# Edge stage of a graph-attention and mixture-of-experts kernel: each gather of source rows waits for the landing of the last but one

## The chip, the core and the metric

The kernel is one program on one core of a Trainium2 chip. A core has five engines that run their own instruction streams and meet through semaphores: PE (TensorE, matmuls), DVE (VectorE), ACT (ScalarE), POOL (GpSimd) and SP (SyncE, which here only issues DMAs); 16 DMA engines move the data. The metric is the device time of one execution in microseconds, lower is better.

## What is computed

A graph layer and a mixture of experts follow each other. Cut to what matters:

```
x = x + gnn(layernorm(x), ...)                       # 3750 nodes x 256, 120000 edges sorted by dst
    feat_all = einsum('ni,rhid->rnhd', inputs, conv_weights)       # 8 relations, 4 heads of 64
    feat_src_e = feat_all[edge_type, edge_src]                     # one row of 256 per edge
    el, er = attn_l . feat_src_e,  attn_r . feat_dst_e             # per head
    e = leaky_relu(el + er, 0.2)
    alpha = softmax of e over the edges with the same dst
    h = segment_sum(alpha * feat_src_e, edge_dst) + h_bias
x = x + ffn(layernorm(x), ...)                       # top 2 of 8 experts, 256 -> 1024 -> 256, gelu
```

## The kernel before

The program has three stages. The **node stage** (to about 243 us) computes the projected rows of all nodes for all 8 relations and writes them to a table `feats` in DRAM, 30720 rows of 260 floats: 256 features and the 4 left logits, 1040 bytes a row. The **edge stage** (243 to about 1885 us) is where the change lies. The **route and expert stage** follows to the end; it uses no gathers from `feats`.

The edge stage cuts the edges into units of 128 and pairs of two units; a pair adds into one tile of 128 destination nodes, and there are 498 pairs. A group is up to 16 pairs (32 units): `SIZES` is 8, then 30 times 16, then 10, so `GROUPS` = 32. A quad is 4 units. Buffers for groups stand threefold (`GBUFS` = 3, r = g modulo 3), so group g uses the buffer of group g - 3.

Each unit's 128 source rows come by one indirect DMA, issued by POOL (`gather_features`, L798), into `gath[:, r, u]`: 128 x 260 floats, 133 KB. POOL issues them in order of group and unit. Ahead of a group it waits for the indices (`idx_ready`, from `meta_columns` on DVE), and ahead of each quad, from group 3 on, for the sums of the pairs that used the same rows three groups ago (`sum_ready`, `freed(g, j)`). `wait_apart` is a wait followed by an increment of a semaphore `carrier` that nobody reads. Every gather increments `gath_in[r]` by 16 when it has landed; `landed(g, r, n)` is the count that this semaphore has when all of group g is there.

Who waits for the gathers: DVE's `logits(g)` (L838), which adds the left logits, columns 256 to 259 of the gathered rows, to the right logits; and SP, once, before it loads the node rows (L784) for the next stage over the rows of a buffer. DVE's `period(g)` does, in a fixed order, the maxima of group g, the scaling of its first rows by alpha (L905, shared with ACT's L1063), the adding of sums into `acc` (L914), the index work for group g + 3, and ends with `logits(g + 1)`. PE's period turns one-hot matrices (L1113), picks right logits (L1138) and sums (`total`, L1154: `psP` from `hot` and `gath`); totals of group g are spread over period g (its first quads, at the end) and period g + 1 (quads 3 to 7). ACT makes the one-hots. Groups are driven by `each_period`: a few first and last ones written out, the others in a hardware loop of three groups.

SP's loads of edge records, 16 of 12 KB a group, run beside the gathers on SP's own DMA queue.

Of the kernel before, what the change touches and what calls it, by code (L numbers as in the profile page):

```python
# [44 lines left out]
BLK = 2  # L45
# [3 lines left out]
GB = 16  # L49
GU = GB * BLK  # L50
assert GU * HEADS == P
SIZES = [8] + [GB] * ((PAIRS - 18) // GB) + [10]
SHORT = GB - SIZES[0]
# [7 lines left out]
GBUFS = 3  # L61
# [93 lines left out]
def wait_apart(pool, sem, value, carrier):  # L155


    pool.wait_ge(sem, value)
    pool.sem_inc(carrier, 1)
# [14 lines left out]
def load_records(nc, sp, sb, edges, meta, g, landed, of=range(GB)):  # L174

    edge_rows = edges.rearrange("t h c e -> (t h) (c e)")
    for b in of:
        if b % 4 == 0:
            starts = nc.values_load_multi_w_load_instructions(
                sb["pair_row"][0:1, bass.ds(g, 1), b:b + 4].rearrange("a g b -> a (g b)"), engines=(mybir.EngineType.SP,),  # L180
                min_val=0, max_val=(CHUNK_ROWS - BLK) * HEADS)[1]
        at = starts[b % 4]
        sp.dma_start(meta[b * BLK * HEADS:(b + 1) * BLK * HEADS], edge_rows[bass.ds(at, BLK * HEADS), :]).then_inc(landed, 16)
# [441 lines left out]
def edge_stage(nc, sb, edges, feats, xb, wr, br):  # L625
# [6 lines left out]
    with ExitStack() as ctx:  # L632
# [6 lines left out]
        def sem(name):  # L639
            return ctx.enter_context(nc.semaphore(name))  # L640
# [9 lines left out]
        reset, cat, idxT, ndlT, typeT = sb["reset"], sb["cat"], sb["idxT"], sb["ndlT"], sb["typeT"]  # L650
# [24 lines left out]
        SLOTS_Q = GU // QUAD  # L675
        LAG = 3
        PQ = QUAD // BLK

        meta_in = sem("meta_in")
        gath_in = [sem(f"gath_in{r}") for r in range(GBUFS)]  # L680
        rows_ready, rowsT_ready, idx_ready = sem("rows_ready"), sem("rowsT_ready"), sem("idx_ready")
        hot_ready, hotT_ready, hotT_copied, er_done = sem("hot_ready"), sem("hotT_ready"), sem("hotT_copied"), sem("er_done")
        e_ready, eT_ready, spread_ready, lv_ready = sem("e_ready"), sem("eT_ready"), sem("spread_ready"), sem("lv_ready")
# [5 lines left out]
        carrier = sem("carrier")  # L689

        def quads(g):

            if not isinstance(g, int):
                return SLOTS_Q
            return SIZES[g] // PQ if 0 <= g < GROUPS else 0

        def pairs_before(g):
            return BASES[g] if isinstance(g, int) else g * GB - SHORT

        def quads_before(g):  # L700
            return BASES[g] // PQ if isinstance(g, int) else g * SLOTS_Q - SHORT // PQ

# [4 lines left out]
        def landed(g, r, n):  # L707

            if isinstance(g, int):
                return 16 * BLK * sum(SIZES[r:g + 1:GBUFS])  # L710
            return 16 * BLK * GB * (n + 1) - (16 * BLK * SHORT if r == 0 else 0)

        def freed(g, j):

            if isinstance(g, int):
                return BASES[g - GBUFS] + min(PQ * j + PQ, SIZES[g - GBUFS])
            return pairs_before(g - GBUFS) + PQ * j + PQ

        def tiles_of(engine, g, j, n):

            numbers = pair_tile[0:1, bass.ds(g, 1), PQ * j:PQ * (j + n)].rearrange("a g b -> a (g b)")
            return nc.values_load_multi_w_load_instructions(
# [3 lines left out]
        def each_period(eng, body, first, last_loop):  # L726


            for g in range(first):
                body(g, g % GBUFS, g // GBUFS)  # L730
            loops = (last_loop + 1 - first) // GBUFS
            with eng.Fori(0, loops) as i:
                for k in range(first, first + GBUFS):
                    body(i * GBUFS + k, k % GBUFS, i + k // GBUFS)
            for g in range(first + GBUFS * loops, GROUPS + 1):
                body(g, g % GBUFS, g // GBUFS)

        def there(g):
            return not isinstance(g, int) or 0 <= g < GROUPS

        LAST_LOOP = GROUPS - 4
        LAST, LAST2 = GROUPS - 1, GROUPS - 2
        ACT_SCALES = [(LAST2, j) for j in range(3, SIZES[LAST2] // PQ)] + [(LAST, j) for j in range(2, SIZES[LAST] // PQ, 2)]
        ACT_Q = (6, 7)
# [21 lines left out]
        with nc.Block() as block:  # L766
            @block.sync
            def _(sp):
                load_records(nc, sp, sb, edges, meta, AHEAD, meta_in)

                def period(g, r, n):
                    if there(g + AHEAD + 1):
                        sp.wait_ge(rows_ready, g + 1)
                        load_records(nc, sp, sb, edges, meta, g + AHEAD + 1, meta_in)

                each_period(sp, period, 2, GROUPS - AHEAD - 2)
                sp.dma_start(sb["wr_sb"][:], wr.rearrange("(k p) e -> p k e", p=P)).then_inc(sb["small_in"], 16)
                sp.dma_start(sb["br_all"][:], br.to_broadcast([P, EXPERTS])).then_inc(sb["small_in"], 16)

                sp.wait_ge(sum_ready, BASES[LAST2])  # L780
                sp.wait_ge(gath_in[LAST % GBUFS], landed(LAST, LAST % GBUFS, 0))
                x_tiles = xb.rearrange("(t p) f -> p t f", p=P)
                for b, (lo, hi) in enumerate(BATCHES_R):
                    sp.dma_start(rows_of_nodes(sb)[:, lo:hi], x_tiles[:, lo:hi]).then_inc(sb["x_in"][b], 16)  # L784

            @block.gpsimd
            def _(pool):
                def gather_features(g, r, n):
                    if not there(g):
                        return  # L790
                    if not isinstance(g, int) or g >= AHEAD:
                        wait_apart(pool, idx_ready, g - (AHEAD - 1), carrier)
                    for j in range(quads(g)):
                        if not isinstance(g, int) or g >= GBUFS:

                            wait_apart(pool, sum_ready, freed(g, j), carrier)
                        for u in range(j * QUAD, (j + 1) * QUAD):
                            pool.indirect_dma_start(gath[:, r, u], None, feats,  # L798
                                                    bass.IndirectOffsetOnAxis(ap=idxT[:, r, u:u + 1], axis=0)).then_inc(gath_in[r], 16)

                each_period(pool, gather_features, GBUFS + 1, GROUPS - 2)

            @block.vector
            def _(dve):
# [28 lines left out]
                def logits(g, r, n):  # L833

                    dve.wait_ge(picked, g * 2 + 2)
                    dve.wait_ge(gath_in[r], landed(g, r, n))
                    e0 = e_sb[:, 0].rearrange("p (u h) -> p u h", h=HEADS)
                    step(dve.tensor_tensor(e0, gath[:, r, :, D:FW], er_e[:], ALU.add))  # L838
                    dve.scalar_tensor_tensor(e_sb[:, 1], e_sb[:, 0], SLOPE, e_sb[:, 0], ALU.mult, ALU.max).then_inc(e_ready, 1)
# [123 lines left out]
                def period(g, r, n):  # L963
# [53 lines left out]
                    if there(g + 1):  # L1017
                        logits(g + 1, rn, n if r < GBUFS - 1 else n + 1)
# [216 lines left out]
def rows_of_nodes(sb):  # L1235

    words = sb["gath"][:, NODE_BUF].rearrange("p u w -> p (u w)")
    return words[:, 0:TILES * D].rearrange("p (t d) -> p t d", t=TILES)
# [816 lines left out]
```

## Time and profile before

| | |
|---|---|
| time, median of 3 runs | 2474.11 us (2470.37 to 2475.55) |
| span of the profiled execution | 2456.4 us |
| time of the profiled execution itself | not given apart; the runs' median lies 17.7 us above the span |
| busy, share of the span: PE, DVE, ACT, POOL | 77%, 43%, 44%, 46% |
| gathers L798 | 996, 954 ns mean, 950.6 us in total |
| DMA queue of POOL (software_dynamic) | 60192 packets, 149.24 MB |

How to read it: the span is from the first to the last instruction of one execution, taken by the hardware profiler, and busy times are parts of it. The 40 slices give the busy share of each engine in tenths. A timeline row gives start and length of an instruction in microseconds, then engine, line, operation and tiles, and in brackets how long the engine idled before it and what ended that. The length of an L798 row is the time in which POOL issues the gather; the rows land later, as packets of the 16 DMA engines. The landing of a gather has no row of its own.

### The profile page before, as it was taken

The page shows a single profiled execution, that of the slowest core. Times are in us where ns is not written, and L with a number is a line of the kernel's source. Part 1 is how long each engine was busy: PE and PEld are TensorE (multiplying, and loading weights), DVE is VectorE, ACT ScalarE, POOL GpSimd, SP SyncE. Part 2 cuts the span into 40 slices and gives each one's busy share as a digit, 9 for nine tenths or more (in the row PEclk, how much of TensorE's full clock was granted, in tenths as well). Part 3 has the DMA queues.
Part 4 walks back from the last instruction along what each step waited for, and adds up shares of the span by engine and source line. Part 5 has one row for each costly group of instructions (what it writes and reads, how often), then busy time and mean ns, then how long its engine had stood idle before and what let it go on. Part 6 is the DMA issues. An engine that isn't in the chain of part 4 may idle for free. (4 is left out here: it accounts for less than half of the span.)

```text
span 2456.4 us, 35279 instructions
## 1 busy us (share of the span) xinstructions
PE 1898.8 (77%) x9138; PEld 1594.8 (65%) x9139; DVE 1062.3 (43%) x3018; ACT 1076.9 (44%) x3259; POOL 1142.0 (46%) x1164
## 2 busy tenths in 40 slices
PE   8999125767767777867777777677877689999998
PEld 7887124656655665656565666565665668999887
DVE  6332013545555555545555555455567532221111
ACT  2222123645555545554555555454656532222221
POOL 4000744556666566666666566656620443122222
PEclk9999556787877768777787777777788689999999
DMA  6443422333333333333333333333312877777774
GB/s 239 189 170 143 109 67 74 84 90 88 90 92 92 88 88 91 90 88 90 88 92 92 89 90 90 92 85 88 91 44 80 282 230 221 248 246 247 241 234 104
DMA packets 121157, 315.51 MB, mean 128 GB/s; under 512 B 27047, under 2 KB 71335, under 8 KB 106180
## 3 DMA queue, kind: packets, MB, share of 16 engines
q0 software_dynamic: 60192, 149.24, 23.4%
q1 hardware_dynamic: 60836, 164.88, 19.3%
q8 instruction: 41, 0.67, 0.1%
q14 instruction: 88, 0.72, 0.1%
HBM read 257.36 MB, written 57.71 MB: 128 GB/s over the span
## 5 line engine op out<-in xcount | busy, mean ns | idle before, releaser
L798 POOL DMA_INDIRECT gath<-feats,idxT x996 | 950.6, 954 | 799.1 <-issue 272.7
L1154 PE MATMUL psP<-gath,hot 128*128 128x260 f32 x1992 | 668.1, 493 | 28.6 <-DVE gath L905 15.1
L1154 PEld LDWEIGHTS psP<-gath,hot 128*128 128x128 f32 x1992 | 469.4, 247 | 123.5 <-issue 35.4
L1113 PE MATMUL psOT<-cst,hot 128*128 128x128 f32 x996 | 196.1, 331 | 346.0 <-ACT hotT L1045 231.9
L1045 ACT COPY hotT<-psOT 128x512 f32<-128x512 f32 x249 | 143.5, 576 | 628.6 <-remote 485.4
L1113 PEld LDWEIGHTS psOT<-cst,hot 128*128 128x128 f32 x996 | 139.7, 171 | 407.2 <-issue 309.0
L1138 PEld LDWEIGHTS psE<-er,hotT 128*128 128x128 f32 x1992 | 309.7, 235 | 48.6 <-issue 44.9
L914 DVE TENSOR_TENSOR acc<-acc,psP 128x260 f32 x498 | 211.0, 424 | 295.3 <-remote 127.9
L1138 PE MATMUL psE<-er,hotT 128*128 x1992 | 309.5, 305 | 31.1 <-issue 19.9
L1035 ACT ACTIVATE hot<-cst,ndlT 128x128 f32<-128x128 f32 x996 | 316.2, 391 | 4.7 <-PEq L325 4.7
L1680 ACT ACTIVATE acc<-psH,w1buf 128x256 f32<-128x256 f32 (+1 forms) x344 | 122.4, 423 | 346.7 <-PE psH L1571 304.3
L1063 ACT ACTIVATE gath<-gath 128x64 f32<-128x64 f32 x1040 | 261.0, 337 | 0.1
L1496 POOL DMA_INDIRECT out<-acc,node x66 | 103.3, 1565 | 335.0 <-DVE acc L1904 178.0
L1571 PE MATMUL psH<-acc,w1buf 128*128 128x256 f32 (+1 forms) x1376 | 241.9, 334 | 4.4 <-issue 2.4
L1587 PE MATMUL psY<-w2buf,acc 128*128 128x256 f32 x1056 | 240.9, 384 | 3.4 <-issue 3.3
L905 DVE TENSOR_TENSOR gath<-gath,psA 128x1024 f32<-128x1024 f32 x184 | 224.5, 1221 | 27.2 <-ACT gath L1075 19.9
L1571 PEld LDWEIGHTS psH<-acc,w1buf 128*128 128x128 f32 x1376 | 217.8, 194 | 24.8 <-DVE acc L1888 2.9
L585 PE MATMUL psF<-wext,xT 128*128 128x264 f32 x960 | 221.1, 388 | 1.1 <-ACT xT L536 1.1
L1587 PEld LDWEIGHTS psY<-w2buf,acc 128*128 128x128 f32 x1056 | 200.0, 193 | 32.4 <-issue 6.8
L585 PEld LDWEIGHTS psF<-wext,xT 128*128 128x128 f32 x960 | 180.7, 191 | 31.6 <-ACT xT L536 1.5
L1038 ACT ACTIVATE hot<-hot 128x512 f32<-128x512 f32 x249 | 156.8, 630 | 38.3 <-remote 25.9
L1888 DVE TENSOR_SCALAR acc<-psX,w1buf 128x256 f32<-128x256 f32 (+1 forms) x86 | 37.5, 478 | 214.8 <-PE psX L1556 186.1
(232 smaller groups left out, 1178.5 us busy)
## 6 DMA issues: line engine op xcount, KB each, us to landing
w1buf<-in_experts SPq DMA_DIRECT2D x43, 1030.0 KB
w2buf<-in_experts SPq DMA_DIRECT2D x43, 1024.0 KB
feats<-frow SPq DMA_DIRECT2D x29, 1040.0 KB, 3.9
gath<-feats,idxT POOLq DMA_INDIRECT x996
meta<-in_edges SPq DMA_DIRECT2D x464, 12.0 KB
acc<-slots_x SPq DMA_DIRECT2D x23, 258.0 KB
gath<-in_b SPq DMA_DIRECT2D x43, 128.0 KB
acc<-slots_x SPq DMA_DIRECT2D x20, 129.0 KB
```

The lines of the kernel that those rows point to most:

```text
L585: ins = pe.matmul(psF[:, n % BUFS, j, 0:W], xT[:, i % LEAD, k], wext[:, k, 2 * pair + j], start=k == 0, stop=k == KD - 1)
L798: pool.indirect_dma_start(gath[:, r, u], None, feats, bass.IndirectOffsetOnAxis(ap=idxT[:, r, u:u + 1], axis=0)).then_inc(gath_in[r], 16)
L905: dve.tensor_tensor(feat, feat, alpha.unsqueeze(3).to_broadcast([P, QUAD, HEADS, HD]), ALU.mult).then_inc(scaled, 1)
L914: dve.tensor_tensor(into[b % PQ], into[b % PQ], psP[:, bank(g, b, r), 0:FW], ALU.add).then_inc(sum_used, 1)
L1035: ins = act.activation(hot[:, r, u], iota, ACT.Square, bias=ndlT[:, r, u:u + 1])
L1038: act.activation(hot[:, r, j * QUAD:(j + 1) * QUAD], hot[:, r, j * QUAD:(j + 1) * QUAD], ACT.Relu, bias=1.0, scale=-1.0).then_inc(hot_read ...
L1063: ins = act.activation(feat, feat, ACT.Copy, scale=gath[:, r, u, D + h:D + h + 1])
L1113: ins = pe.transpose(psOT[:, k * P:(k + 1) * P], hot[:, r, j * QUAD + k], ident)
L1138: ins = pe.matmul(psE[:, u * W % 512:u * W % 512 + W], hotT[:, j % 2, k * P:(k + 1) * P], tables[k // BLK], start=True, stop=True)
L1154: ins = pe.matmul(psP[:, bank(g, b, r), 0:FW], hot[:, r, u], gath[:, r, u], start=u % BLK == 0, stop=u % BLK == BLK - 1)
L1571: ins = pe.matmul(psH[:, bank(n, g), at * slots(n):(at + 1) * slots(n)], w1(n, k, m), xeT[:, n % 2, k, 0:slots(n)], start=k == 0, stop=k = ...
L1587: ins = pe.matmul(psY[:, y_bank(n, j), 0:D], hT[:, n % 2, m, j * P:(j + 1) * P], w2(n, m), start=m == 0, stop=m == KH - 1)
```

## The change

The semaphore of each buffer becomes two (`FLYING` = 2): gather u raises the one of number u modulo 2. From the third gather of a group on, POOL waits before gather u until the semaphore of that number shows that gather u - 2 of the same group has landed. The first two gathers of a group have no such wait. The counts of `landed` are halved, and DVE and SP wait for both semaphores.

```diff
+        FLYING = 2
-        gath_in = [sem(f"gath_in{r}") for r in range(GBUFS)]
+        gath_in = [[sem(f"gath_in{r}_{q}") for q in range(FLYING)] for r in range(GBUFS)]
...
-                return 16 * BLK * sum(SIZES[r:g + 1:GBUFS])
-            return 16 * BLK * GB * (n + 1) - (16 * BLK * SHORT if r == 0 else 0)
+                return 16 * BLK // FLYING * sum(SIZES[r:g + 1:GBUFS])
+            return 16 * BLK // FLYING * GB * (n + 1) - (16 * BLK // FLYING * SHORT if r == 0 else 0)
+
+        def landed_before(g, r, n):
+
+            if isinstance(g, int):
+                return 16 * BLK // FLYING * sum(SIZES[r:g:GBUFS])
+            return 16 * BLK // FLYING * GB * n - (16 * BLK // FLYING * SHORT if r == 0 else 0)
...
-                sp.wait_ge(gath_in[LAST % GBUFS], landed(LAST, LAST % GBUFS, 0))
+                for q in range(FLYING):
+                    sp.wait_ge(gath_in[LAST % GBUFS][q], landed(LAST, LAST % GBUFS, 0))
...
                         for u in range(j * QUAD, (j + 1) * QUAD):
+                            if u >= FLYING:
+
+                                wait_apart(pool, gath_in[r][u % FLYING], landed_before(g, r, n) + 16 * (u // FLYING), carrier)
                             pool.indirect_dma_start(gath[:, r, u], None, feats,
-                                                    bass.IndirectOffsetOnAxis(ap=idxT[:, r, u:u + 1], axis=0)).then_inc(gath_in[r], 16)
+                                                    bass.IndirectOffsetOnAxis(ap=idxT[:, r, u:u + 1], axis=0)).then_inc(
+                                                        gath_in[r][u % FLYING], 16)
...
-                    dve.wait_ge(gath_in[r], landed(g, r, n))
+                    for q in range(FLYING):
+                        dve.wait_ge(gath_in[r][q], landed(g, r, n))
```

No instruction changes its place; waits are added between them. On POOL, at the head of the hardware loop (a group in buffer 1; `L158` is register and wait work), before:

```order
L158 ISA [waits idx_ready]
L798 DMA gath<-feats,idxT 128x260 [waits sum_ready]
L798 DMA gath<-feats,idxT 128x260 x3
L158 REGISTER_ALU
L798 DMA gath<-feats,idxT 128x260 [waits sum_ready]
L798 DMA gath<-feats,idxT 128x260 x3
```

and now:

```order
L158 ISA [waits idx_ready]
L809 DMA gath<-feats,idxT 128x260 [waits sum_ready]
L809 DMA gath<-feats,idxT 128x260
L158 ISA
L809 DMA gath<-feats,idxT 128x260 [waits gath_in1_0]
L809 DMA gath<-feats,idxT 128x260 [waits gath_in1_1]
L158 REGISTER_ALU
L158 REGISTER_ALU [waits sum_ready]
L809 DMA gath<-feats,idxT 128x260 [waits gath_in1_0]
L809 DMA gath<-feats,idxT 128x260 [waits gath_in1_1]
```

Every gather from the third on has a wait of its own, in turn on the two semaphores of the buffer, where one in four had one. On DVE, the end of a period in the loop, before:

```order
L905 TENSOR_TENSOR gath<-gath,psA 128x4x256 [waits sum_used]
L835 REGISTER_ALU
L836 ISA [waits picked]
L838 TENSOR_TENSOR e_sb<-gath,er_e 128x128 [waits gath_in0]
L152 REGISTER_ALU
L839 SCALAR_TENSOR_TENSOR e_sb<-e_sb 128x128 [waits v_step_edges]
```

and now:

```order
L918 TENSOR_TENSOR gath<-gath,psA 128x4x256 [waits sum_used]
L847 REGISTER_ALU
L849 ISA [waits picked]
L851 TENSOR_TENSOR e_sb<-gath,er_e 128x128 [waits gath_in0_1,gath_in0_0]
L152 REGISTER_ALU
L852 SCALAR_TENSOR_TENSOR e_sb<-e_sb 128x128 [waits v_step_edges]
```

The logits stand where they stood and wait for two semaphores instead of one.

## Rows read from the trace of the kernel before

**Rows 1.** The 40 slices of the page, 61.4 us each: busy tenths.

```profile
PE   8999125767767777867777777677877689999998
...
POOL 4000744556666566666666566656620443122222
...
DMA  6443422333333333333333333333312877777774
```

**Rows 2.** Timeline of DVE: start, length, line, operation, tiles, [idle before, releaser].

```profile
377.82 0.42 DVE L914 TENSOR_TENSOR acc<-acc,psP 128x260 f32 x1 [1.50 <-PE psP L1154]
...
438.95 0.28 DVE L838 TENSOR_TENSOR e_sb<-gath,er_e 128x128 f32<-128x128 f32 x1
...
839.51 0.29 DVE L838 TENSOR_TENSOR e_sb<-gath,er_e 128x128 f32<-128x128 f32 x1
...
1038.05 0.28 DVE L838 TENSOR_TENSOR e_sb<-gath,er_e 128x128 f32<-128x128 f32 x1
...
1857.48 0.29 DVE L838 TENSOR_TENSOR e_sb<-gath,er_e 128x128 f32<-128x128 f32 x1
...
1885.22 0.68 DVE L1754 TENSOR_TENSOR gath<-gath,acc 128x512 f32<-128x512 f32 x1
...
2442.34 0.35 DVE L1904 TENSOR_SCALAR acc<-acc,gate 128x256 f32<-128x256 f32 x1
```

**Rows 3.** Timeline of POOL, the first 80 gathers and the one after.

```profile
243.56 1.14 POOL L798 DMA_INDIRECT gath<-feats,idxT  x1 [185.65 <-POOLq L325]
...
248.83 0.95 POOL L798 DMA_INDIRECT gath<-feats,idxT  x1 [0.30 <-issue]
...
343.12 0.95 POOL L798 DMA_INDIRECT gath<-feats,idxT  x1 [0.30 <-issue]
378.38 0.95 POOL L798 DMA_INDIRECT gath<-feats,idxT  x1 [34.31 <-PE psP L1154]
```

**Rows 4.** Timeline of POOL: mid-stage, group 14's first and last, the last gather.

```profile
925.40 0.95 POOL L798 DMA_INDIRECT gath<-feats,idxT  x1 [0.30 <-issue]
...
933.58 0.95 POOL L798 DMA_INDIRECT gath<-feats,idxT  x1 [3.45 <-DVE ndlT L216]
...
980.06 0.95 POOL L798 DMA_INDIRECT gath<-feats,idxT  x1 [0.31 <-issue]
...
1806.63 0.95 POOL L798 DMA_INDIRECT gath<-feats,idxT  x1 [0.30 <-issue]
```

**Rows 5.** Waits of POOL, 500 to 1700 us: total, times, longest.

```profile
POOL gath L798 <- PE psP L1154: 139.5, 71, 3.9
POOL gath L798 <- remote: 105.7, 40, 3.3
```

**Rows 6.** Stretches: length, busy (count) of the engines, PEclk, DMA share, GB/s.

```profile
345.50:345.60 0.10, 0.00 (x0) 0.00 (x0) 0.00 (x0) 0.00 (x0) 0.00 (x0) 0.50 0.02 0
345.60:345.70 0.10, 0.00 (x0) 0.00 (x0) 0.00 (x0) 0.00 (x0) 0.00 (x0) 0.50 0.01 0
345.70:353.00 7.30, 0.00 (x0) 0.00 (x0) 0.00 (x0) 0.00 (x0) 0.00 (x0) 0.50 0.00 0
...
982.40:982.50 0.10, 0.00 (x0) 0.00 (x0) 0.00 (x0) 0.00 (x0) 0.00 (x0) 1.00 0.03 0
...
1809.50:1809.70 0.20, 0.20 (x2) 0.20 (x1) 0.19 (x1) 0.20 (x1) 0.00 (x0) 0.50 0.01 0
```

**Rows 7.** Stretches of the last stage, the same columns.

```profile
2443.30:2443.40 0.10, 0.10 (x2) 0.09 (x1) 0.00 (x0) 0.00 (x0) 0.00 (x0) 1.00 0.03 0
2443.40:2444.50 1.10, 1.10 (x7) 0.97 (x6) 0.00 (x0) 0.00 (x0) 0.00 (x0) 1.00 0.00 0
```

**Rows 8.** Timeline of POOL, the scatter that waited for a landing.

```profile
2444.51 1.56 POOL L1496 DMA_INDIRECT out<-acc,node  x1 [3.02 <-DMA out<-acc,node]
```

**Rows 9.** DMA issues: count, KB each, us from issue to landing.

```profile
gath<-xb SPq DMA_DIRECT2D x1, 1792.0 KB, 13.0
```

**Rows 10.** Stretch of 300 us in mid-stage, columns as in rows 6.

```profile
800.00:1100.00 300.00, 224.28 (x1026) 182.28 (x1026) 157.13 (x426) 160.56 (x498) 183.09 (x192) 0.76 0.33 89
```

## The prediction

> **What bounds the kernel now.** I read the busy shares and the 40 slices first, for where the edge stage lies and who works in it. In the slices [rows 1], a slice being 61.4 us, the stage runs from the fifth (243 us) to the thirty-first; PE is busy 6 to 7 tenths, POOL 6, the 16 DMA engines 3. No engine is full. What repeats is a period of one group: the logits L838 are computed once for each of the 32 groups, and for groups 2, 10, 14 and 31 they start at 438.95, 839.51, 1038.05 and 1857.48 [rows 2], so a period is (1038.05 - 438.95)/12 = 49.9 us, and other stretches give much the same: (839.51 - 438.95)/8 = 50.1. It is set by PE, DVE and ACT handing on to each other; the gathers are not in it. The rows of POOL show why. At the start it issues 80 gathers without a pause, each 0.95 us and 0.30 of gap, 1.257 us from one to the next ((343.12 - 248.83)/75) [rows 3]. In mid-stage it works in bursts: the 32 gathers of group 14 start at 933.58 to 980.06 [rows 4] and are wanted by the L838 at 1038.05 [rows 2], 55 us after they landed. Of 1200 us in mid-stage POOL idles 140 for PE to free rows and 106 for a releaser not named, the rest in the 0.30 gaps [rows 5]. So a gather may take 49.9/32 = 1.56 us before POOL becomes the bound, and it takes 1.26.
>
> **The time of one gather, from start to landing to next start.** This is the number on which all hangs, since the change lets gather u start only when u - 2 has landed. No row gives it, so I put it together from two.
> First, start to last packet. The gather of 343.12 is followed by none for 35 us. The data end by 345.5, and the last small packets (no bytes to speak of, those that raise the semaphore) are in 345.6 to 345.7; then nothing [rows 6]. That is 2.5 us. The one of 980.06, in mid-stage, has its last in 982.4 to 982.5: 2.4 us. The last one of all, 1806.63 [rows 4], trails into 1809.5 to 1809.7: 3.0 us [rows 6]. I take 2.5.
> Second, last packet to the start of the waiting gather. The nearest row is a scatter of the last stage that waits on POOL for the landing of an earlier scatter: small packets end in 2443.3 to 2443.4, nothing is under way after them, and POOL starts at 2444.51, DVE having been done at 2442.69 [rows 2, 7, 8]: 1.1 us, 1.2 from the other edge. It is the same engine, the same kind of instruction and a DMA's semaphore, so I take it. From below, if a landing is heard as soon as a matmul's end: DVE starts at 377.82 and POOL at 378.38 on the same release [rows 2, 3], 0.56 us later.
> So the loop is L = 2.5 + 1.1 = 3.6 us, with ends 2.4 + 0.6 = 3.0 and 3.0 + 1.2 = 4.2. As two are in the air, two gathers go per L: 1.8 us each, over the 1.56 that are free.
> Here the Trainium skill speaks for no effect: DMA: Bandwidth & Descriptors, section "Anatomy of one DMA — SWDGE (gpsimd) path", fits 2.0 us plus bytes/436e9 per DMA. For 133 KB that is an estimated 2.3 us, half of it 1.15, less than POOL's own 1.26; this case's packets alone already take 2.5 with the wake-up still to come, and I go by them.
>
> **Part by part.**
> 1. The 932 new waits on POOL (30 of each 32; the first two gathers of a group wait for nothing new). A group of m pairs has 2m gathers and takes (m - 1) L + 2 x 1.257. The sizes sum to 498 over 32 groups, so from the first start the POOL chain is 466 L + 80.4 us. With L = 3.6: 1677.6 + 80.4 = 1758; the last gather starts at 243.56 + 1758 - 1.26 = 2000.3 and lands 2.8 later (2.5 and a little for the semaphore), at 2003.1. POOL does not wait for rows to be freed on the way: group 3 starts at 384 where its rows are free at 378.38 [rows 3], and it only falls behind from there, by 56.5 (15 L + 2.5) against 49.9 us a group.
> 2. Who waits for it. DVE's logits stand in DVE's row, and behind them the whole next period. Group 3 now lands at 442, wanted at about 489: 47 us of margin, losing 6.6 a group, gone after seven. From **group 10 on, about 840 us** [rows 2], L838 waits for the landing. From there the period is 56.5 us, and L838 of group 31 starts at 2003.1 instead of 1857.48: **+145.6 us**. POOL's end rules, not the last period: group 31 follows group 30 by 9 L + 2.5 = 34.9 us where the two L838 now stand 32.6 apart.
> 3. What comes after. From that L838 to the end of the span are 2456.4 - 1857.5 = 598.9 us, unchanged. The node rows' loads on SP, issued when the group before is summed, must now await the last landing and go out with it. The longest takes 13.0 us [rows 9] and the first use of them, L1754, comes 27.7 us after L838 (1885.22) [rows 2]: hidden by 14 us. Without that cover it would be 13.
> 4. Semaphore counting: a carrier increment beside each wait, register work in the loop. Both come while POOL's sequencer waits anyway; in mid-stage the gathers that already have such a wait, when it is met, show the same 0.30 gap (925.40, the first of its four) [rows 4]. From above, a tenth of the gap for each of 466 pairs would be 14 us; I take 0. DVE's and SP's second wait: 32 and 1, at nothing, since both semaphores are full within 1.3 us of each other; at most 0.3 each, 10 us.
> Sum: 2456.4 + 145.6 = 2602 for the span. The three runs' median 2474.1 is 17.7 above the profiled span (the page gives no separate time for that execution), which I carry over: **2620 us**. Each 0.1 us of L is 46.6 us of time.
>
> **Rivals.**
> A, not slower. The margin is used up only if 466 L > 1857.5 - 2.8 - 243.6 - 79.1, so L must be over 3.29 us; 3.16 is where a group takes 49.9 us. If a landing in SBUF is heard much sooner than one in DRAM, at the 0.56 of a matmul's release, L is 3.0: everything is hidden, 2474 us. For it: the row I took for 1.1 is a write into DRAM. Against it: 0.56 counts from where DVE starts, not from a packet, and half of the difference to 1.1 already brings L to 3.3, the point itself. The page's fit ends here too. 10%, of which 2% for a little faster: fewer gathers beside SP's 464 loads of edge records, which nobody waits for; nothing in the rows says they collide (DMA 3 tenths).
> B, stragglers decide. Each landing is the slowest of 16 engines. If the 3.0 of 1806.63 is the rule with traffic about, L = 4.1: 2620 + 0.5 x 466 = 2853 us. One of three samples says so, but mid-stage says 2.4. 7%.
> C, PE's clock. The granted clock is 0.76 in 800 to 1100 [rows 10], between its levels of 2.4 GHz and of 1.2, the 0.50 that stands where PE idles [rows 6]. PE is busy 224 of 300 us, 37 of a period's 50. Six more idle us in each could bring the grant down; if it fell below 0.65, 37 would grow to 44 and the period's own chain over 56.5. At 0.60 it is 37 x 0.76/0.60 + 13 = 60: 3.5 us more in 20 periods, 2690 us. 5%.
> D, as forecast: 78%.
> That the change does nothing (a wait whose count is reached already) I give no chance: each wait asks for the 16 of gather u - 2 on that gather's own semaphore, on top of all that earlier groups raised.
>
> **How the numbers follow.** About 0.2% (5 us) is what a measurement of this kernel can tell from no change. Slower by more: D, B, C and nothing of A, 0.90; within: 0.08; faster: 0.02. The time is D's. Its range is L from 3.4 to 3.8, 2527 to 2713; C lies in it; outside are most of A and B and a few in a hundred of D, so 2530 to 2710.
>
> **What would show it.** In the changed profile POOL's gathers should alternate 0.30 and some 1.4 us of idle, waiting for the DMA; about 56 us from group to group; a last gather near 2000; L838 without wait before 800 us and with several us, for the landing, after about 840; PE's share down to some 72%. The waits for PE psP on POOL should be gone. I am wrong if gathers of a pair follow each other in less than 3.3 us (A), over 4 (B), or if L838 never waits on gath though the time has grown (C).

## The result, and the profile after

| | before | after |
|---|---|---|
| median | 2472.24 us (2468.71 to 2475.55) | 2633.8 us (2631.28 to 2635.17) |
| ratio | | **1.065**, 95% interval 1.063 to 1.068 |
| span of the profiled execution | 2456.4 us | 2632.2 us |
| busy share PE, DVE, ACT, POOL | 77%, 43%, 44%, 46% | 68%, 40%, 41%, 43% |

Forecast were 2620 us and slower. The changed kernel's page, slices of 65.8 us: PE has gone down to 4 to 6 tenths in the edge stage, from mostly 6 to 8 in [rows 1], and the DMA engines to 2.

```profile
PE   8998455656545666644566654456565688999998
...
POOL 4001555555555555555555555555554245222212
PEclk9998567777777777777777777777777688999999
DMA  6533222222222222222222222222222486877774
```

POOL's timeline, three stretches of the changed kernel (start and length in us, then the instruction, in brackets the idle time before it and what ended it). This answers to [rows 3] and [rows 4].

```profile
243.90 1.14 POOL L809 DMA_INDIRECT gath<-feats,idxT  x1 [185.65 <-POOLq L325]
245.35 0.99 POOL L809 DMA_INDIRECT gath<-feats,idxT  x1 [0.30 <-issue]
247.84 0.95 POOL L809 DMA_INDIRECT gath<-feats,idxT  x1 [1.51 <-DMA gath<-feats,idxT]
...
1003.26 0.95 POOL L809 DMA_INDIRECT gath<-feats,idxT  x1 [1.32 <-DMA gath<-feats,idxT]
1004.54 0.95 POOL L809 DMA_INDIRECT gath<-feats,idxT  x1 [0.33 <-issue]
1006.99 0.95 POOL L809 DMA_INDIRECT gath<-feats,idxT  x1 [1.50 <-DMA gath<-feats,idxT]
...
2033.09 0.95 POOL L809 DMA_INDIRECT gath<-feats,idxT  x1 [0.33 <-issue]
```

The gathers go in pairs, 0.30 and some 1.4 us of idle in turn, and the waits for the landing are where they were expected. From the first start to the last are 1789.2 us = 466 L + 79.2, so **L = 3.67 us** on average.

DVE's timeline of the changed kernel at its logits L851 (L838 before), for groups 0, 1, 4, 29 and 31; this answers to [rows 2].

```profile
274.19 0.29 DVE L851 TENSOR_TENSOR e_sb<-gath,er_e 128x128 f32<-128x128 f32 x1 [15.98 <-DMA gath<-feats,idxT]
...
331.14 0.29 DVE L851 TENSOR_TENSOR e_sb<-gath,er_e 128x128 f32<-128x128 f32 x1 [27.36 <-DMA gath<-feats,idxT]
...
505.90 0.29 DVE L851 TENSOR_TENSOR e_sb<-gath,er_e 128x128 f32<-128x128 f32 x1 [22.70 <-DMA gath<-feats,idxT]
...
1943.53 0.29 DVE L851 TENSOR_TENSOR e_sb<-gath,er_e 128x128 f32<-128x128 f32 x1 [22.02 <-DMA gath<-feats,idxT]
...
2036.24 0.29 DVE L851 TENSOR_TENSOR e_sb<-gath,er_e 128x128 f32<-128x128 f32 x1 [3.66 <-DMA gath<-feats,idxT]
```

Here two things don't fit the prediction. L851 waits from **group 0** on, not from group 10; its waits are 712 us in all. And the first L851 starts at 274.2 where the first L838 of before started at 312.6. A period is (1943.53 - 505.90)/25 = 57.5 us, of which over 22 are this wait: the rest of the period needs only some **35 us**, not the 50 of before. With the gathers restrained, everybody else is quicker. With groups numbered from 0, the logits start at

| group | 0 | 1 | 3 | 5 | 10 | 20 | 31 |
|---|---|---|---|---|---|---|---|
| before | 312.6 | 383.0 | 489.7 | 590.1 | 839.5 | 1335.4 | 1857.5 |
| after | 274.2 | 331.1 | 448.5 | 566.8 | 853.2 | 1426.2 | 2036.2 |

so that the changed kernel is 41 us ahead at group 3, still 23 at group 5, and behind at group 10. (The profiled execution of before is a quick one, some 10 us below the quickest of its four measured runs, so that these leads are rather too small than too large.)

Where the time had gone in the kernel before shows at the stage's start, while POOL issues its 80 gathers in a row [rows 3]. The timeline of the kernel before, all engines, cut to the hand-off of the right logits and of a transposed one-hot:

```profile
268.33 1.91 PE L1138 MATMUL psE<-er,hotT 128*128 x8 [12.85 <-issue]
...
270.08 1.12 PE L1113 MATMUL psOT<-cst,hot 128*128 128x128 f32 x4
...
311.01 0.69 DVE L827 TENSOR_TENSOR er_all<-psE,typeT 128x512 f32<-128x512 f32 x1 [67.34 <-remote]
...
322.21 0.58 ACT L1045 COPY hotT<-psOT 128x512 f32<-128x512 f32 x1 [50.35 <-remote]
```

The same hand-off in the changed kernel:

```profile
253.30 3.46 PE L1151 MATMUL psE<-er,hotT 128*128 x16
...
256.80 0.69 DVE L839 TENSOR_TENSOR er_all<-psE,typeT 128x512 f32<-128x512 f32 x1 [12.80 <-PE psE L1151]
```

Before, PE's matmuls for the right logits end at 270.2 (PE runs no further L1138 until 323.82), and DVE, which by the code waits for nothing else here, starts at 311.0: 41 us later. After, it is 0.04 us. ACT's copy at 322.21 comes as late, 51 us behind the end of PE's transposes (271.2). The trace names no releaser for such waits; it calls them "remote". The waits of 500 to 1700 us, of the kernel before:

```profile
ACT hotT L1045 <- remote: 318.5, 49, 13.0
...
DVE acc L914 <- remote: 106.9, 46, 6.3
```

and of the changed kernel, where no row says "remote":

```profile
ACT hotT L1058 <- PE psOT L1126: 523.1, 76, 22.5
DVE e_sb L851 <- DMA gath<-feats,idxT: 478.2, 21, 26.6
...
POOL gath L809 <- DMA gath<-feats,idxT: 322.8, 242, 3.4
```

ACT's 523 us are idle time downstream of L851's wait, not late hand-offs. Summed over PE, DVE and ACT, the "remote" rows of this stretch are 688 us before and nothing after. I call them the **late hand-offs** from here on: work of PE is done, and the engine that waits for it starts microseconds later. The sums are of all idle time before such starts, so a part of each is honest waiting. PE itself has no "remote" row; where it waits for ACT it starts at once (268.33, when ACT's copy of 267.61 ends at 268.19).

What such a hand-off looks like in mid-stage, in the kernel before (the timeline of 889 to 902 us, cut to the rows that matter):

```profile
889.97 1.06 PE L1113 MATMUL psOT<-cst,hot 128*128 128x128 f32 x4
...
892.39 3.81 PE L1154 MATMUL psP<-gath,hot 128*128 128x260 f32 x8
...
896.97 0.95 POOL L798 DMA_INDIRECT gath<-feats,idxT  x1 [0.30 <-issue]
...
900.15 0.58 ACT L1045 COPY hotT<-psOT 128x512 f32<-128x512 f32 x1 [9.67 <-remote]
900.41 0.99 DVE L914 TENSOR_TENSOR acc<-acc,psP 128x260 f32 x2 [3.07 <-remote]
...
901.12 0.95 POOL L798 DMA_INDIRECT gath<-feats,idxT  x1 [3.20 <-remote]
```

ACT's copy wants the transposes that end at 891.03. PE goes on to 16 later matmuls, up to 896.2, and still ACT starts only at 900.15; DVE and POOL, which wait for sums of PE, start within 1 us of it. POOL's last issue had ended 2.2 us before, at 897.92. This is typical: of the 107 "remote" waits of over 2 us that ACT and DVE have in 500 to 1700 us, 93 end in a gap of over 0.4 us between two instructions of POOL, and such gaps are 22% of the time. By itself this doesn't say which is cause and which effect, since POOL, too, waits for PE in these gaps. (The profile models the ends of matmuls; whether the work ends late or only the news of it, it doesn't tell.)

PE's matmuls are quicker after the change too: the sums L1154 took 493 ns on average before, and 448 after.

```profile
L1154 PE MATMUL psP<-gath,hot 128*128 128x260 f32 x1992 | 668.1, 493 | 28.6 <-DVE gath L905 15.1
...
L1167 PE MATMUL psP<-gath,hot 128*128 128x260 f32 x1992 | 589.2, 448 | 2.9 <-DVE gath L918 2.5
```

The theory to test: POOL issuing gathers without a pause delays PE's hand-offs, and the change removed this, but at 3.67/2 us a gather it made POOL's own chain longer than what it freed. Rivals: fewer gathers in the air (traffic) is what helps, or fewer bytes.

### The profile page after: what moved, and what is told of

It reads as the page before. It is cut to its first block and busy times, and to the rows that moved or that the text cites. A ratio compares the mean times of both kernels' runs of the same rounds, so it can differ in the third digit from the quotient of the medians.

```text
span 2632.2 us, 36482 instructions
## 1 busy us (share of the span) xinstructions
PE 1781.2 (68%) x9138; PEld 1526.8 (58%) x9139; DVE 1058.7 (40%) x3018; ACT 1077.2 (41%) x3259; POOL 1141.1 (43%) x1164
## 5 line engine op out<-in xcount | busy, mean ns | idle before, releaser
L1167 PE MATMUL psP<-gath,hot 128*128 128x260 f32 x1992 | 589.2, 448 | 2.9 <-DVE gath L918 2.5
L1232 PE MATMUL psS<-cst,e_sb 128*128 128x128 f32 x31 | 14.7, 475 | 689.6 <-DVE e_sb L852 689.6
L1167 PEld LDWEIGHTS psP<-gath,hot 128*128 128x128 f32 x1992 | 421.6, 222 | 72.5 <-DVE gath L918 4.3
L1232 PEld LDWEIGHTS psS<-cst,e_sb 128*128 128x128 f32 x31 | 5.6, 182 | 693.1 <-DVE e_sb L852 693.1
L1151 PEld LDWEIGHTS psE<-er,hotT 128*128 128x128 f32 x1992 | 293.5, 224 | 26.7 <-issue 24.5
L1151 PE MATMUL psE<-er,hotT 128*128 x1992 | 291.7, 295 | 14.6 <-DVE er_e L841 14.2
L851 DVE TENSOR_TENSOR e_sb<-gath,er_e 128x128 f32<-128x128 f32 x32 | 9.4, 292 | 712.3 <-DMA gath<-feats,idxT 712.3
L1126 PE MATMUL psOT<-cst,hot 128*128 128x128 f32 x996 | 189.3, 322 | 44.8 <-ACT hotT L1058 27.3
```

The costliest lines, as they stand in the source:

```text
L1126: ins = pe.transpose(psOT[:, k * P:(k + 1) * P], hot[:, r, j * QUAD + k], ident)
L1151: ins = pe.matmul(psE[:, u * W % 512:u * W % 512 + W], hotT[:, j % 2, k * P:(k + 1) * P], tables[k // BLK], start=True, stop=True)
L1167: ins = pe.matmul(psP[:, bank(g, b, r), 0:FW], hot[:, r, u], gath[:, r, u], start=u % BLK == 0, stop=u % BLK == BLK - 1)
```

## The experiments

Each median stands to that of the kernel before on the same chip (2473.6 to 2476.1 us).

**How many are in the air.** The changed kernel with the number generalised, for 3, 4 and 1; each number has its own semaphore and count.

```diff
-        FLYING = 2
+        FLYING = 3
...
```

> FLYING = 3: three semaphores per buffer, gather u waits for u - 3. A gather that follows a landing starts 3.67 us after the one it waited for (466 such steps fit the last gather's 2033.09 us of the changed kernel), so at POOL's own 1.257 us per gather 3.67/1.257 = 2.9 are in the air: the waits are mostly met and a group takes 32 x 1.26 to 1.28 = 40 to 41 us. Theory H (the other engines' own work in a period is only about 35 us, as the 57.5 us less the 23 us wait of the changed kernel say, and it is stretched to 50 us by gathers issued back to back, because then the increments of semaphores by PE and others arrive late): if a restraint at three is enough to keep hand-offs quick, POOL's chain sets the end, 243.9 + 996 x 1.28 + 2.8 + 596 = about 2120 us. If it is not enough, because three in the air is what the kernel before has anyway, 2474 us as before. Rival P (the period's work is 50 us in itself, and the 23 us wait is an artefact of order): 2474 us, L838 never waiting.

Measured: 2481.6 us, ratio 1.003 (1.001 to 1.005).

> FLYING = 4. 4 x 1.257 = 5.0 us is over the 3.67 us, so every wait is met when it is reached: this is the kernel before plus 896 waits that hold nothing up. Theory H: 2474 us, like before; if waits as such (POOL's sequencer stopping to look) helped, it would be nearer to the time of three in the air. Rival P: 2474 us.

Measured: 2485.6 us, ratio 1.004 (1.002 to 1.006).

> FLYING = 1: each gather of a group waits for the one before it. The chain is 964 loops and 32 x 1.257 us. If the loop is the 3.67 us that two in the air show, the last gather starts at 243.9 + 964 x 3.67 + 40 = 3822 us and the span is about 3822 + 2.8 + 596 = 4420 us; if part of the 3.67 comes from the other gather in the air (theory: none, the rows of before give 2.5 to the last packet and 1.1 to the next start), it is shorter by 96 us for each 0.1. L838 then waits some 80 us of a 117 us period, the rest being the others' own 35 us.

Measured: 4353 us, in a single run; it lies under the forecast 4420 because L is 3.60 us and not 3.67. With 3 in the air the new wait almost never holds (L/3 is 1.22 us, POOL takes 1.257 for a gather): the waits of POOL for landings are 15 us of 1200. So POOL issues as before, the first L838 starts at 325.3, and the "remote" waits are 716 us. The ratio of 1.004 with 4 in the air bounds what the waits themselves cost: some 10 us for all of them together, and by the interval at most 14. With one in the air (POOL's timeline) L is seen by itself, 3.57 and 3.55 us here, 3.60 on average over the stage:

```profile
1000.29 0.95 POOL L812 DMA_INDIRECT gath<-feats,idxT  x1 [2.55 <-PE psP L1170]
1003.86 0.95 POOL L812 DMA_INDIRECT gath<-feats,idxT  x1 [2.61 <-DMA gath<-feats,idxT]
1007.41 0.95 POOL L812 DMA_INDIRECT gath<-feats,idxT  x1 [2.60 <-DMA gath<-feats,idxT]
```

In the same kernel a period is 112.9 us (groups 5 to 30), of which L854 waits 78.0 on average, so again some 35 us are all that the rest needs.

**Restraint at the start alone.** The waits of the change only in groups 0 to 2.

```diff
-                            if u >= FLYING:
+                            if u >= FLYING and isinstance(g, int) and g < GBUFS:
```

> FLYING = 2, but only the gathers of groups 0 to 2, the 80 that nothing else holds back, wait; from group 3 on they go freely as before. Theory H: the start gains as in the changed kernel (its L838 of group 1 at 331 us where before has 383), the rest runs at 50 us per group: L838 of group 2 at about 390 instead of 439, total 2474 - 49 = 2425 us. Rival P: the start is not held up by gathers, 2474 us or a few us more.

Measured: 2477.4 us, ratio 1.001 (0.998 to 1.003). The logits start at 275.1, 333.3 and 390.9 as in the changed kernel, but those of group 3 at 488.4, as in the kernel before (489.7): 97 us lie between groups 2 and 3, and the waits of 390 to 490 us show in what:

```profile
ACT hotT L1061 <- remote: 62.4, 3, 49.5
DVE lv L874 <- remote: 40.4, 1, 40.4
```

The forecast of 2425 us took it that the start's gain would stay; it didn't. As soon as the gathers are free again, they are issued in a row, and the late hand-off comes back. It follows the gathers' pace, not the place in the stage.

**Fewer bytes.** The kernel before, where from group 4 on each gather brings 20 floats a row.

```diff
-                            pool.indirect_dma_start(gath[:, r, u], None, feats,
+                            w = FW if isinstance(g, int) and g <= GBUFS else 20
+                            pool.indirect_dma_start(gath[:, r, u, 0:w], None, feats if w == FW else short_rows,
```

> The kernel before, but from group 4 on a gather brings 20 floats per row (80 bytes, of other rows) where it brought 260: features and logits of these groups are what is left in the buffer, so that part of the edge stage is not computed. POOL's work, the 128 packets and the 16 semaphore increments per gather stay, the bytes fall to a thirteenth. Theory H in the form that the issue (POOL's back-to-back instructions, their packets and increments) does the harm: still about 50 us a period, 2474 us. Rival B (the bytes do it, by loading the DMA engines or the memories): the period falls to POOL's own 40.2 us, 243.9 + 996 x 1.257 + 2.8 + 596 = 2095 us.

Measured: 2474.5 us, ratio 1.001 (0.998 to 1.004), the "remote" waits at 695 us, with 11 GB/s moved in mid-stage instead of 90. The bytes are not the cause.

**Pauses without any wait for a landing.** The kernel before, and ahead of every 2nd (4th, 8th) gather a memset of one scratch column on POOL and a wait for that memset's own increment.

```diff
+                            if u % 2 == 0:
+                                pool.memset(blank[:], 0.0).then_inc(paced, 1)
+                                wait_apart(pool, paced, paced_before(g) + u // 2 + 1, carrier)
                             pool.indirect_dma_start(gath[:, r, u], None, feats,
```

> The kernel before with no wait for landings; instead POOL writes one column of a scratch tile ahead of every second gather and waits for its own increment, which costs about 0.1 + 0.78 - 0.30 us: 1.257 and 1.9 in turn, 1.57 us per gather on average, 50.3 us a group. In the air are 1.8 to 2.3. Theory H in the form that the rate of issue matters: L838 waits for landings from the start, 243.9 + 996 x 1.57 + 2.8 + 596 = 2406 us. In the form that only a wait for landings helps, and rival P: 2474 us or a little over.

Measured: **2414.9 us, ratio 0.977** (0.973 to 0.982), span 2406.2.

> As spaced2, but POOL writes its scratch column and waits for that only ahead of every fourth gather. Of spaced2 two gathers take 3.11 us, so the pause is worth 0.6 us; four take 4 x 1.257 + 0.6 = 5.63 us, 1.407 each, 45.0 us a group. Theory H (gathers issued back to back hold up the other engines' hand-offs; their own work is 35.4 us a period, the 50.3 of spaced2 less its 14.9 us wait): if one pause in four is enough to let the hand-offs through, POOL's chain still sets the end and the span is 243.9 + 996 x 1.407 + 2.8 + 596 = 2244 us. If it is not enough, L838 stops waiting for landings and the time lies between that and 2474 us. Rival S (the memset and its wait help by themselves, not the room they leave): between 2415 and 2474 us.

Measured: 2444.5 us, ratio 0.990 (0.986 to 0.994), span 2439.5 where full relief would have given 2244.

> The same ahead of every eighth gather: eight take 10.66 us, 1.332 each, 42.6 us a group. With relief in full 243.9 + 996 x 1.332 + 2.8 + 596 = 2169 us; with none 2474 us. Theory H expects part of the relief only, since eight gathers in a row are what a burst of the kernel before has: between 2250 and 2474 us.

Measured: 2483.2 us, ratio 1.003 (1.001 to 1.006), no relief where some was forecast.

POOL's timeline with a pause ahead of every 2nd gather: 1.26 and 1.85 us from one gather to the next in turn, the second with 0.79 us in which POOL waits.

```profile
999.54 0.95 POOL L808 DMA_INDIRECT gath<-feats,idxT  x1 [0.30 <-issue]
1000.49 0.11 POOL L806 MEMSET blank<- 128x1 f32 x1
1001.39 0.95 POOL L808 DMA_INDIRECT gath<-feats,idxT  x1 [0.79 <-POOL blank L806]
1002.65 0.95 POOL L808 DMA_INDIRECT gath<-feats,idxT  x1 [0.30 <-issue]
```

Its waits of 500 to 1700 us have 10 us of "remote" instead of 688, and L848 waits for the landing as in the changed kernel, for less:

```profile
ACT hotT L1055 <- PE psOT L1123: 408.5, 79, 12.8
...
DVE e_sb L848 <- DMA gath<-feats,idxT: 356.9, 24, 16.4
...
POOL gath L808 <- POOL blank L806: 290.1, 367, 0.8
```

356.9/24 is 14.9 us of 50.3 a period, which again leaves 35. So no landing need be waited for: a pause of 0.6 us over the usual gap, every second gather, takes the late hand-offs away, and the period is then POOL's own, 16 x (1.257 + 1.857) = 49.8 us. Every fourth does little, every eighth nothing.

One objection has to be met. In mid-stage the kernels without late hand-offs (the changed one, one in the air, a pause per two) are just those in which POOL's chain sets the period, and the others have time to spare while they wait for it. The start of the stage answers it: there POOL waits for no other engine in either kernel and PE has the same work, and DVE's first L827 (L837 with the pauses) starts at 311.0 without them and at 257.2 with one per two.

**How many gathers in a row, or how much room in all.** One pause ahead of every 3rd; and two pauses, one right behind the other, ahead of every 4th.

```diff
+                            if u % 4 == 0:
+                                for turn in range(2):
+                                    pool.memset(blank[:], 0.0).then_inc(paced, 1)
+                                    wait_apart(pool, paced, 2 * (paced_before(g) + u // 4) + turn + 1, carrier)
```

> As the kernel before, but ahead of every fourth gather POOL takes two pauses of 0.60 us one right behind the other (each a memset of one scratch column and a wait for its own increment), so the mean room per gather is the same 1.557 us as with one pause ahead of every second gather, and the pauses lie as far apart as in the kernel with one pause ahead of every fourth (2439.5 us of span, 2444 us median). Theory of the mean room (what relieves PE's increments is how many gathers POOL issues in a given time): span 2406 us, median near 2415, a period of 50.3 us in which L839 waits some 15 us for landings, and hardly any wait put down to 'remote'. Rival, the length of the unbroken run (increments get through only in a pause, and two gathers are the longest run that does not delay them): four gathers in a row hold them as in the kernel with one pause per four, so the span is 2430 to 2460 us with the waits put down to 'remote' of that kernel.

Measured: 2439.4 us, ratio 0.986 (0.982 to 0.989), span 2429.5, just under the rival's 2430 to 2460; "remote" waits 757 us.

> As the kernel before, but with one pause of 0.60 us ahead of every third gather (gathers 0, 3, ... 30 of a group): a mean of 1.46 us per gather. If increments came through freely, POOL's chain alone would set 243.9 + 996 x 1.257 + 343 x 0.60 + 599 = 2301 us of span, and the period's own work of about 35 us would hide in POOL's 46.8 us. Theory (relief falls off between one pause per two and one per four): the period is no longer POOL's but that of the delayed hand-offs, so the span lies above 2301 us; between the 2406 of one per two and the 2439 of one per four, 2380 to 2440, if the relief falls off steadily. Rival (a threshold between three and four): 2301 to 2340 us.

Measured: 2422.2 us, ratio 0.977 (0.975 to 0.980), span 2428.5; "remote" waits 657 us.

The late hand-offs of two pauses ahead of every 4th are where they were (its waits of 500 to 1700 us):

```profile
ACT hotT L1056 <- remote: 382.9, 97, 10.1
```

This kernel was meant to decide between the two theories, by giving four in a row the same mean room as one pause per two gathers. POOL's timeline shows that it didn't:

```profile
1029.95 0.12 POOL L807 MEMSET blank<- 128x1 f32 x1
1030.23 0.10 POOL L807 MEMSET blank<- 128x1 f32 x1 [0.15 <-issue]
1031.12 0.95 POOL L809 DMA_INDIRECT gath<-feats,idxT  x1 [0.79 <-issue]
```

The second memset starts 0.15 us after the first, so that the second pause adds 0.25 us and not 0.60. Four gathers then take 3 x 1.257 + 2.11 = 5.88 us, 1.47 each, which is the mean of one pause per three (1.457) and not of one per two (1.557). What the five kernels show is that relief in mid-stage needs more than one pause per three. Three readings of it stand, and no run parts them: that three gathers in a row are too many, that a mean of 1.47 us is too quick, or that three in the air at once are too many. As to the last, a gather takes some 2.5 us to its last packet and, by the profile of the kernel with one in the air, 2.8 to its landing; three in a row start within 2.51 us, so that a third can start beside two that are not in yet, and with a pause ahead of every 2nd it can't. So the rival "fewer in the air" is not out: only the bytes are.

Where the gains lie is seen from the starts of the logits:

| | group 0 | group 3 | group 5 | us a group, 5 to 30 | group 31 |
|---|---|---|---|---|---|
| before | 312.6 | 489.7 | 590.1 | 49.4 | 1857.5 |
| every 2nd | 270.7 | 420.3 | 521.3 | 50.3 | 1810.9 |
| every 3rd | 268.6 | 451.3 | 559.6 | 49.2 | 1820.9 |
| every 4th | 268.2 | 470.0 | 570.7 | 49.5 | 1841.2 |
| every 4th, two | 268.5 | 418.6 | 554.5 | 50.1 | 1839.1 |
| every 8th | 298.6 | 481.8 | 583.8 | 50.7 | 1884.6 |

Nearly all that these kernels win on the profiled execution of before, they win in the first groups: 69 us by group 5 with a pause ahead of every 2nd, and 31 with one ahead of every 3rd. That execution is a quick one; the medians give 61 and 53 us. For every 3rd, then, some 20 us of the gain can't be placed. In mid-stage all run at about 50 us a group: with a pause ahead of every 2nd gather because POOL takes that long, in the others with the late hand-offs still there. The relief in mid-stage is real (35 us of work a period instead of 50), but the pauses that buy it eat it.

**POOL busy with something else instead of waiting.** The memset stays, the wait asks for the memset before it, long done. One column ahead of every gather; 256 columns ahead of every second.

```diff
+                            if u % 2 == 0:
+                                if not (isinstance(g, int) and g == 0 and u == 0):
+                                    wait_apart(pool, paced, paced_before(g) + u // 2, carrier)
+                                pool.memset(blank[:], 0.0).then_inc(paced, 1)
```

> As the kernel before, with a memset of one scratch column (0.115 us) on POOL ahead of every gather; it waits only for the memset before it, which is done long since, so POOL never stands still for its own semaphore: some 0.15 us of work that is no gather between two gathers, a mean of about 1.41 us per gather. POOL's chain alone would then give 243.9 + 996 x 1.41 + 599 = 2247 us of span, and the rest of the period needs some 35 us of POOL's 45. Theory (only a stretch in which POOL waits lets PE's increments through, and it must be some tenths of a microsecond long): no relief, 2450 to 2490 us, with waits put down to 'remote' as in the kernel before. Rival (any break between two gathers serves, so the unbroken run, here one gather, is all that counts): 2250 to 2350 us with L839 or POOL's own order setting the period.

Measured: 2496.4 us, ratio 1.008 (1.005 to 1.010), "remote" waits 705 us.

> As the kernel before, with a memset of 256 scratch columns (about 0.1 + 0.21 = 0.31 us) on POOL ahead of every second gather; it waits only for the memset before it, long done. The mean is about 1.43 us per gather, like the kernel with a short memset ahead of every gather, but in one piece per two gathers. POOL's chain alone would give 243.9 + 996 x 1.43 + 599 = 2267 us. Theory (a pause in which POOL waits for an event is what lets increments through): no relief, 2450 to 2490 us. Rival (POOL busy with something that is no gather serves as well as POOL waiting): relief between one pause per two gathers and full, 2270 to 2410 us.

Measured: 2469.3 us, ratio 0.998 (0.996 to 0.999), "remote" waits 621 us.

POOL's timeline of the first shows that it tested less than meant: the memset lies in what was the gap of 0.30 us, and a gather still comes every 1.26 us, not 1.41.

```profile
1002.49 0.11 POOL L808 MEMSET blank<- 128x1 f32 x1
1002.79 0.96 POOL L809 DMA_INDIRECT gath<-feats,idxT  x1 [0.19 <-POOL blank L808]
1003.74 0.12 POOL L808 MEMSET blank<- 128x1 f32 x1
1004.05 0.96 POOL L809 DMA_INDIRECT gath<-feats,idxT  x1 [0.19 <-POOL blank L808]
```

In the second the gaps between the end of a gather and the start of the next are 0.30 and 0.49 us in turn, a mean of 1.355 us a gather and not 1.43:

```profile
1003.18 0.96 POOL L809 DMA_INDIRECT gath<-feats,idxT  x1 [0.30 <-issue]
1004.14 0.33 POOL L808 MEMSET blank<- 128x256 f32 x1
1004.63 0.96 POOL L809 DMA_INDIRECT gath<-feats,idxT  x1 [0.16 <-issue]
```

There is no relief worth the name in either, as the first theory says; the first lies 6 us above its 2450 to 2490, slower than the kernel before. But the gaps are 0.49 us at most, against 0.90 in the kernel that helps, so these runs don't tell whether POOL has to stand still or only has to leave a longer gap. That stays open.

## Why the prediction was right, and where it was not

**The loop of one gather.** Forecast 3.6 us (2.5 to the last packet, 1.1 to the next start), measured 3.67 with two in the air and 3.60 with one. It carried the forecast, and with one in the air both of its terms can be read: of the gather that starts at 1003.86 the last small packets lie in 1006.16 to 1006.36 (DMA engines 2% busy, 0 GB/s, and 0% in the 0.5 us behind), 2.3 to 2.5 us after its start, and the next starts at 1007.41, 1.05 us or a little more after that. The 0.07 are 466 x 0.07 = 33 us. Rival A (3.0, not slower) and B (4.1) are out, and the Trainium skill's fit for a DMA of this kind (DMA: Bandwidth & Descriptors, "Anatomy of one DMA — SWDGE (gpsimd) path"), by which nothing would have waited, is too short here: an estimated 2.3 us for 133 KB, where the profile with one in the air has 2.8 us from issue to landing (median) and 3.60 to the next start.

**The sum.** The last group's logits were forecast for 2003.1 and start at 2036.2 (+33.1, the term just named); from there to the end of the span are 596.0 us instead of 598.9 (-2.9); the median lies 1.6 us above the profiled span and not 17.7 (-16.1). 2620 + 33.1 - 2.9 - 16.1 = 2634. That the error is 14 us and not 30 is luck, and due to the last of these: the profiled execution of the kernel before was a quick one, and its distance to the median is no constant to carry over.

**The new bound.** POOL's chain sets the time, 57.5 us a group (56.5 forecast), PE's share is 68% (72 forecast), and the node rows' loads stayed hidden, as the 596.0 show. Rival C, PE's clock: the granted clock is 0.73 to 0.75 in mid-stage after, 0.76 in [rows 10] before, and with one gather in the air 0.60 to 0.65, between PE's levels of 1.2 and 2.4 GHz; the rest of a period then still takes 35 us, and the sums L1170 446 ns each. It decides nothing.

**The step that failed** is in the first part: that the period of 50 us "is set by PE, DVE and ACT handing on to each other; the gathers are not in it". The first half is right and the second is not. The hand-offs were late because of the gathers (688 us of "remote" waits before, 10 with a pause per two), and the period's own work is 35 us. From this came the second wrong statement, a margin of 47 us that is used up at group 10, with no wait of L838 before; in fact it waits from group 0, since everyone else arrives early. The total did not suffer, as POOL's chain runs from 243.9 us to the last landing in either picture and doesn't depend on the margin. But no rival said that holding gathers back could speed up the other engines. The rows for it were in the trace of before: "remote" as the releaser of the largest wait of ACT (318.5 us), and 106 us of POOL's [rows 5], which I passed over as "a releaser not named". The program runs on one core, so such a row is a question: which producer was it, and when was it done?

**What it was worth.** The restraint had gained 41 us by group 3. Between groups 5 and 30 it cost 198 us: 1999.96 - 566.77 after, against 1824.87 - 590.13 before, 57.3 and 49.4 us a group.

## What to carry to other kernels

A limit of F transfers in the air costs L/F per transfer, with L from start to start of a gather that waits for a landing (3.6 us here, for 133 KB); it is free only while L/F is below what the issuing engine takes anyway (3.67/3 = 1.22 against 1.257 us here), so work this out before F is chosen. When the other engines' waits show no releaser while one engine issues without a pause, try a pause in that engine's stream before any restraint that waits for landings, and read in the timeline what the pause really costs (here two in a row cost 0.85 us, not 1.20): 0.6 us ahead of every second or third gather gave 2.3% on the kernel before and beats both kernels of this case. And compare when each period starts, not only its length: here the gain that the profiles show lay in the first five groups.

## What the runs showed of the hardware

Gathers issued every 1.257 us without a pause go with late hand-offs from PE: 41 us in one piece at the start of the stage, some 690 us of idle time summed over DVE and ACT in 1200 us of mid-stage. It is nearly gone with POOL waiting 0.79 us ahead of every second gather (10 us), and still there with one such pause per three (657), per four (664) and per eight (723), with rows of 80 bytes instead of 1040 (695) and with 3 or 4 in the air (716, 701). In mid-stage, then, relief sets in between one pause per three gathers and one per two; whether the run without a pause, the mean time per gather or the number in the air decides was not told apart. At the start of the stage pauses per three or four already bring the first logits forward from 312.6 to 268. The late hand-offs are all of PE's work, to DVE, ACT and POOL; in mid-stage 93 of the 107 over 2 us end while POOL issues nothing. The duration of a matmul changes with it: L1154's is 493 ns before, 499 with a pause per three gathers and 449 per two, at much the same granted clock (0.76, 0.77 and 0.77 in 500 to 1700 us). What in the issue of a gather does this was not found; which of POOL's instructions, its packets or the landing's increments is at work would need a kernel that has one without the others. A wait of POOL for the increment of its own memset takes 0.79 us from the memset's end to the gather's start, but only 0.15 to the start of another memset.
